# Eight sign levels instead of seven in the second quantiser, and the output copies moved from VectorE to ScalarE

## The reference, cut to what matters

```python
def _act_quant(x):
    scale = QB / jnp.maximum(jnp.max(jnp.abs(x), axis=-1, keepdims=True), EPS)   # QB = 127
    q = jnp.clip(jnp.round(x * scale), -QB - 1, QB) / scale
def _weight_quant(w):
    scale = 1.0 / jnp.maximum(jnp.mean(jnp.abs(w)), EPS)
    q = jnp.clip(jnp.round(w * scale), -1.0, 1.0) / scale
h = x * rsqrt(mean(x * x) + EPS) * w_norm
value, gate = split(_act_quant(h) @ _weight_quant(w_gv))     # hidden 8192 each
u = value * silu(gate)
out = _act_quant(u) @ _weight_quant(w_out)                   # 8192 -> 2048
x = layernorm(x + (x + out))                                 # w_norm is ones
```

## Time and profile before

| what | us |
|---|---|
| median of two runs | 7970.94 (7932.42 and 8009.45) |
| the profiled execution, its own time | 7965.22 |
| its span on the slowest core (core 6) | 7963.7 |
| spans of the other cores | 7869.0 to 7954.0 |
| VectorE busy / ScalarE busy / TensorE busy | 4085.7 / 3093.0 / 3355.5 |
| start of the last stage's first load of `ub2` | 5035.63 |

### The profile page before, as it was taken

The page is one execution under the profiler, slowest core; times in us unless marked ns, Lnnn a source line. Parts: engine busy times, 40 slices in busy tenths (PEclk is TensorE's granted clock), DMA queues, the critical chain, the costliest instruction groups (busy, mean ns, idle before and its releaser), DMA issues.

```text
span 7963.7 us, 48961 instructions; the slowest of 8 cores (7869.0 to 7963.7 us)
## 1 busy us (share of the span) xinstructions
PE 3355.5 (42%) x12882; PEld 1355.7 (17%) x13138; DVE 4085.7 (51%) x3369; ACT 3093.0 (39%) x3030; POOL 180.3 (2%) x343
## 2 busy tenths in 40 slices
PE   2100021120228888888889300000542715446186
PEld 0000000000014333333333100000210202112032
DVE  3600036658464444444444333677777676677612
ACT  2444421221323333333333455455554354354400
POOL 2000000000000000000000000000000000000000
PEclk7555555555569999999999655555765757667576
DMA  6776610010112222222222465112433415234232
GB/s 154 256 256 210 188 52 21 21 42 0 40 48 96 96 95 96 95 96 96 96 96 99 134 198 185 38 63 63 139 100 122 132 64 164 92 104 139 83 122 100
DMA packets 217460, 853.69 MB, mean 107 GB/s; under 512 B 34656, under 2 KB 34656, under 8 KB 159840
## 3 DMA queue, kind: packets, MB, share of 16 engines
q1 hardware_dynamic: 120240, 604.05, 22.7%
q10 hardware_dynamic: 64512, 167.80, 5.6%
q0 software_dynamic: 32432, 78.70, 4.1%
HBM read 694.24 MB, written 167.77 MB: 108 GB/s over the span
## 4 chain that ended last, share of the span: by engine, by line
DVE 45%; ACT 19%; DMA 17%; PE 8%; issue 6%; POOL 1%; ACTq 1%; DVEq 1%; SPq 0%; POOLq 0%
DVE zt L80 16%; DMA ub<-u_sp 5%; DMA wmean<-wgvt 5%; ACT wqt L80 4%; ACT wqs L80 4%; DMA wmean<-woutT 3%; PE pout L1323 3%; DVE res L80 3%; DVE paby L80 3%; ACT wabs L80 3%; DVE Mx L80 2%; DVE mq L80 2%; DVE o_ts L80 2%; DVE sg_t L80 2%; DVE gc_t L80 2%
## 5 line engine op out<-in xcount | busy, mean ns | idle before, releaser
L1323 PE MATMUL pout<-q_r,qo_r 128*128 128x512 bf16 x4012 | 1045.2, 428 | 1129.9 <-DMA qo_r<-qo_sp 598.5
L1017 PE MATMUL pvg<-q,qwv 128*128 128x512 bf16 x4014 | 1029.3, 412 | 378.4 <-DVE u_r L80 212.4
L80 DVE SCALAR_TENSOR_TENSOR zt<-mq,zt 128x1024 f32<-128x1024 f32 x768 | 941.2, 1225 | 138.6 <-DVE zt L80 136.8
L80 ACT ACTIVATE mq<-zt,pbh 128x1024 f32<-128x1024 f32 x768 | 881.9, 1148 | 197.2 <-DVE zt L80 194.8
L1022 PE MATMUL pvg<-q,qwg 128*128 128x512 bf16 x4014 | 928.9, 382 | 4.4
L1323 PEld LDWEIGHTS pout<-q_r,qo_r 128*128 128x128 bf16 x4096 | 437.6, 107 | 1741.5 <-issue 1635.3
L80 ACT ACT_TABLE_LOAD x77 | 98.8, 1283 | 1579.9 <-DVE q L80 404.3
L1017 PEld LDWEIGHTS pvg<-q,qwv 128*128 128x128 bf16 x4096 | 423.3, 104 | 954.4 <-issue 566.1
L80 ACT ACTIVATE wabs<-wmean 128x2048 f32<-128x2048 f32 (+1 forms) x256 | 379.6, 1483 | 473.3 <-DMA wmean<-wgvt 265.8
L1022 PEld LDWEIGHTS pvg<-q,qwg 128*128 128x128 bf16 x4096 | 402.8, 98 | 490.2 <-issue 29.5
L80 ACT ACTIVATE sg_t<-gc_t 128x512 f32<-128x512 f32 x256 | 161.2, 630 | 558.5 <-DVE gc_t L80 558.5
(11 more groups left out here) (146 smaller groups left out, 3889.6 us busy)
## 6 DMA issues: line engine op xcount, KB each, us to landing
wmean<-wgvt SPq DMA_DIRECT2D x128, 1024.0 KB, 6.0
wld<-wgvt SPq DMA_DIRECT2D x128, 1024.0 KB, 4.9
qo_r<-qo_sp SPq DMA_DIRECT2D x128, 1024.0 KB, 5.7
wmean<-woutT SPq DMA_DIRECT2D x128, 512.0 KB, 4.2
u_sp<-u_r ACTq DMA_DIRECT2D x64, 1024.0 KB, 4.4
wo_r<-woutT SPq DMA_DIRECT2D x128, 512.0 KB, 3.8
ub<-u_sp POOLq DMA_DIRECT2D x256, 256.0 KB, 5.3
qo_sp<-qo_t ACTq DMA_DIRECT2D x128, 256.0 KB, 2.9
```

The lines of the kernel that those rows point to most:

```text
L80: r = f(*a, **kw)
L1017: t.matmul(pvg[:, 2 * q * TS:(2 * q + 1) * TS], qwv[:, r * 2048 + k * 128:r * 2048 + (k + 1) * 128], q1[:, (ts * DC + k) * TS:(ts * DC + k ...
L1323: last = t.matmul(pout[:, d * TS:(d + 1) * TS], qo_r[:, base + d * 128:base + (d + 1) * 128], rhs, start=(j == 0), stop=(j == HC - 1))
```

## The change

Three edits, all in the last stage.

1. The level with weight 0.5 is done like the other seven: `HYB_S` gets an eighth weight, the loops run to 8, and VectorE's `tensor_scalar` (`is_ge`) and `tensor_tensor` (subtract) of each lane go. The bias of the copy to `q2c` changes from -1.0 to -0.5.
2. The eight copies `o_ts <- pout` of the first half are ScalarE's: the callback is called in ScalarE's program of the quantiser ahead of pair 8, and TensorE waits for ScalarE's semaphore.
3. The eight copies of the second half, in the epilogue, are ScalarE's as well; VectorE waits for them.

```diff
-    HYB_S = [-64.0, -32.0, -16.0, -8.0, -4.0, -2.0, -1.0]
+    HYB_S = [-64.0, -32.0, -16.0, -8.0, -4.0, -2.0, -1.0, -0.5]
...
             for p in range(NP):
-                if mid_cb is not None and p == NP // 2:
-                    mid_cb(v)
                 for lane in range(2):
...
-                for k in range(7):
+                for k in range(8):
                     for lane in range(2):
                         c0, c1 = lane * 2 * TS, (lane + 1) * 2 * TS
-                        v.wait_ge(sA.h, ab + 16 * p + 2 * k + lane + 1)
+                        v.wait_ge(sA.h, ab + 18 * p + soff(p) + 2 * k + lane + 1)
...
-                    v.tensor_scalar(out=mq2[:, c0:c1], in0=zt2[:, c0:c1],
-                                    scalar1=-0.5, scalar2=1.0,
-                                    op0=ALU.is_ge, op1=ALU.mult)
-                    v.tensor_tensor(out=zt2[:, c0:c1], in0=zt2[:, c0:c1],
-                                    in1=mq2[:, c0:c1], op=ALU.subtract)
...
         @SCA
         def _(sc, ts=ts, vb=vb, ab=ab):
             for p in range(NP):
-                vo = voff(p)
-                for k in range(7):
+                if mid_cb is not None and p == NP // 2:
+                    mid_cb(sc)
+                for k in range(8):
...
-                                  in_=mq2[:, c0:c1], func=AF.Copy, bias=-1.0)
+                                  in_=mq2[:, c0:c1], func=AF.Copy, bias=-0.5)
...
                 if dg == 1:
-                    t.wait_ge(sV.h, dg1_gate)
+                    t.wait_ge(sA.h, dg1_gate)
...
-        def cb(v):
-            v.wait_ge(sMM.h, f2_m0 + HC)
+        def cb(sc):
+            sc.wait_ge(sMM.h, f2_m0 + HC)
             if ts > 0:
-                v.wait_ge(sOut.h, 16 * DC * ts)
+                sc.wait_ge(sOut.h, 16 * DC * ts)
             for d in range(8):
-                v.tensor_copy(out=o_ts[:, d * TS:(d + 1) * TS],
-                              in_=pout[:, d * TS:(d + 1) * TS])
+                sc.copy(out=o_ts[:, d * TS:(d + 1) * TS],
+                        in_=pout[:, d * TS:(d + 1) * TS])
...
-        @VEC
-        def _(v, ts=ts, f2_m0=f2_m0):
-            v.wait_ge(sMM.h, f2_m0 + 2 * HC)
+        @SCA
+        def _(sc, ts=ts, f2_m0=f2_m0):
+            sc.wait_ge(sMM.h, f2_m0 + 2 * HC)
             for d in range(8):
-                v.tensor_copy(out=o_ts[:, (8 + d) * TS:(9 + d) * TS],
-                              in_=pout[:, d * TS:(d + 1) * TS])
-        tok_ev2 = sV.n
+                sc.copy(out=o_ts[:, (8 + d) * TS:(9 + d) * TS],
+                        in_=pout[:, d * TS:(d + 1) * TS])
+        tok_ev2 = sA.n
```

More of the change, by code:

```diff
@@ L1177, in emit_q2_slice, with soff @@
         vb, ab = sV.n, sA.n
-        def voff(p):
+        def soff(p):
             return 8 if (mid_cb is not None and p >= NP // 2) else 0
@@ L1182, in emit_q2_slice @@
             pp, lane = divmod(u, 2)
-            vfin[(ts, u)] = vb + 22 * pp + voff(pp) + 21 + lane
+            vfin[(ts, u)] = vb + 20 * pp + 19 + lane
         sl = slice(ts * TS, (ts + 1) * TS)
@@ L1228, in _ @@
                     c0, c1 = lane * 2 * TS, (lane + 1) * 2 * TS
-                    v.tensor_scalar(out=mq2[:, c0:c1], in0=zt2[:, c0:c1],
-                                    scalar1=-0.5, scalar2=1.0,
-                                    op0=ALU.is_ge, op1=ALU.mult)
-                    v.tensor_tensor(out=zt2[:, c0:c1], in0=zt2[:, c0:c1],
-                                    in1=mq2[:, c0:c1], op=ALU.subtract)
-                for lane in range(2):
-                    c0, c1 = lane * 2 * TS, (lane + 1) * 2 * TS
                     v.scalar_tensor_tensor(
@@ L1238, in _ @@
                         in1=ub2[:, c0:c1], op0=ALU.mult, op1=ALU.add)
-        assert sV.n == vb + 22 * NP + (8 if mid_cb is not None else 0)
+        assert sV.n == vb + 20 * NP
         @SCA
@@ L1243, in _ @@
             for p in range(NP):
-                vo = voff(p)
-                for k in range(7):
+                if mid_cb is not None and p == NP // 2:
+                    mid_cb(sc)
+                for k in range(8):
                     for lane in range(2):
                         c0, c1 = lane * 2 * TS, (lane + 1) * 2 * TS
-                        sc.wait_ge(sV.h, vb + 22 * p + vo
+                        sc.wait_ge(sV.h, vb + 20 * p
                                    + (1 + lane if k == 0 else 2 * k + 1 + lane))
@@ L1265, in _ @@
                         in_=q2c[:, lane * 1024:(lane + 1) * 1024]))
-        assert sA.n == ab + 16 * NP
+        assert sA.n == ab + 18 * NP + (8 if mid_cb is not None else 0)
     prev_next_ok = None
@@ L1374, in _ @@
             def _(g):
-                g.wait_ge(sV.h, _ev)
+                g.wait_ge(sA.h, _ev)
                 sLG.inc(g.dma_start(out=draw, in_=o_ts[:]), 16)
@@ L1380, in _ @@
         def _(v, tok_ev2=tok_ev2, tok_lb=tok_lb, c2sl=c2sl, ts=ts):
-            v.wait_ge(sV.h, tok_ev2)
+            v.wait_ge(sA.h, tok_ev2)
             v.wait_ge(sLb.h, tok_lb)
@@ L1486, in build_program @@
     for ts in range(NTS):
-        dg1_gate = sV.n + (22 * NP // 2 + 8 if ts + 1 < NTS else 8)
+        dg1_gate = sA.n + (18 * (NP // 2) + 8 if ts + 1 < NTS else 8)
         f2_m0 = emit_f2_loads_mms(ts, dg1_gate)
@@ L1491, in build_program, with _ @@
         else:
-            @VEC
-            def _(v, ts=ts, f2_m0=f2_m0, cb=mk_evdg0(ts, f2_m0)):
-                cb(v)
+            @SCA
+            def _(sc, ts=ts, f2_m0=f2_m0, cb=mk_evdg0(ts, f2_m0)):
+                cb(sc)
         emit_f2_epilogue(ts, f2_m0)
```

## The result

The changed kernel takes 7834.22 us, median of 11 runs (7810.64 to 7885.10), against 7914.71 us for the kernel before, median of 10 (7902.97 to 8009.45), two of which are the two shown ahead of the prediction. The ratio is 0.9891, with a 95% interval from 0.9854 to 0.9928. The forecast ratio was 7881 / 7965.2 = 0.9894. The forecast time, 7881, is 47 us too high, and its range (7838 to 7932) misses the measured median by 4 us.

A forecast was written before the change was run, and what follows sets the result against it. The prediction took a serial loop of VectorE's levels and a load per pair as the bound. Its terms, -93.4 + 0 + 8.0 + 1.5 = -83.9 us, took 7965.2 to 7881 us, range 7838 to 7932.

The forecast's parts named there:

- What bounds the kernel: Slice quantiser: a serial loop of VectorE's levels, then a load, over 64 pairs; idle time at the load 419.6 us.
- Part 1: Eighth sign level in the quantiser: 1.46 us saved a pair, 93.4 us over 64 pairs.
- Part 2: Copies moved to ScalarE in the middle of three slices: 0 us, bounds -0.4 and +2.4 for each.
- Part 3: Epilogue copies on ScalarE: 2.7 us later three times, +8.0; in the last product and last epilogue +0.75 each, +1.5.
- The sum: Whole kernel: -93.4 + 0 + 8.0 + 1.5 = -83.9 us.
- The level: Whole kernel: the profiled execution's 7965.22 us taken as the base from which the gain was subtracted, giving 7881.
- B: ScalarE's new duties cost more: table loads around the middles and a smaller eighth-level gain, 7898 us; chance 0.07.
- C: Bare last product: TensorE's clock stays lower after the longer pause, 82 us per half, 8045 us with both; chance 0.02.
- A: Quantiser loop: `ub` loads slowed by packed weight traffic; each landing 1.46 us later would give 7975 us; chance 0.06.
- One of my signs of being wrong: Last product: the prediction is wrong if its second half is not near 136 us.

The follow-up runs named there:

- both later groups: Two later sets of runs, each on one chip beside the unchanged kernel before, whose median was 7942.05 us (19 runs) and 7943.44 us (7 runs).

## Why the prediction was right and where it was wrong

**What bounds the kernel: right.** A serial loop of VectorE's levels and one load. Two buffers took the load out of it and 344 us with it.

**Part 1, -1.46 us a pair: right.** The two operations of the eighth level stand 1.40 apart as forecast, and `ACT mq` releases 3.1 us in 896 operations. That ScalarE's work costs nothing was a claim on 0.25 us of room; without the `Sign` a pair is 0.14 shorter, the hand-over alone.

**Part 2, the middles at 0: right.** 0.5 us won at slice 1's, no table load. The 0.2 I had worked out was too small because I took 0.72 us a copy from an early row; it is 0.66.

**Part 3, +2.7 per epilogue and +0.75 twice: right in kind, too large.** Measured +2.1 and +0.3, again from 5.30 us instead of 5.8 for eight copies. The five added loads are there, each with 1.28 us ahead of its copies. The Trainium skill ("ScalarE: Activation LUTs", "What ACT_TABLE_LOAD costs") adds a drain of about 1380 ns to the load for every switch of set. No such time shows in these rows: a copy begins 1.29 us after its load does, and in the epilogue the load begins 0.49 us after the end of `q2c`.

**The sum, -83.9 us: right, as far as it can be told.** The two comparisons of the changed kernel give 80.5 and 104.5 us less than the kernel before, ratios of 0.9891 and 0.9874; -83.9 of 7965 is 0.9895 and lies in both intervals. With the terms as the rows measured them (+2.1 three times, +0.3 twice, and three times the -0.5 that was read at slice 1's middle) the sum would have been -88.

**The level: wrong.** The step that failed is in the sum and the range: "The profiled execution took 7965.22 ... I say 7881", and then the range centred there, as the two runs "lie 39 us to either side of their median, and I have no reason for less around mine". The level was 50.5 us above the 7914.71 which ten runs of the kernel before gave, and the gain I took off was 3.4 us larger than the one measured there; the two leave the 47 us of error. The stated bounds are not what that working gives either: 39 us to either side of 7881 and of B's 7898 would be 7842 and 7937. What the level held was a stage at a reduced pace on two cores, and there was reason to see it in the views I had, the spans and mean granted clocks of the cores of that execution:

```profile
core 0: 7905.6 us, clock 0.693
...
core 4: 7896.7 us, clock 0.671
core 5: 7916.0 us, clock 0.671
core 6: 7963.7 us, clock 0.678
core 7: 7954.0 us, clock 0.679
```

Cores 6 and 7 stand 38 us and more above the other six. The mean clock does not tell them apart from cores 4 and 5; the row of the last product does, with 0.81. I read that row as the kernel's pace, mostly at the 2.4 GHz level with a start at 1.2, and built rival C on a further fall. It was a reduced pace already: core 6 stays at 0.81 in the stretch from 7800 to 7840 us, 151 matmuls in 40 us where core 4 does 187 at 1.00 from 7720 to 7760, and on the other six cores T was some 50 us shorter. Of those six the slowest is core 5, and 7916.0 + 1.5 - 83.9 = 7833.6 would have been the forecast, beside 7834.22 measured. That it meets it within a us is luck: the undisturbed profile taken later would have given 7929.3 - 83.9 = 7845.4 by the same rule, and in both later groups the median of the kernel before was 28 us above its first one. That part of the level I can't explain.

**The rivals.** A (the load takes it back): no. On the mean of the cores the wait is 416.4 and 426.9 us in the two profiles of before, 414.5 with the eighth level alone, and 428.6 and 438.8 in the two of the full change, where the loads of the middles are no longer behind VectorE's copies. B: no; there is no load in the middles, and the pace is 1.40. C: the pause grew to 6.98 us and the half after it ran at 0.99; refuted as an effect of this change, but what it fears, a lower granted clock in the bare last product, is what cost the profiled execution 50 us. One of my signs of being wrong came out by this: the second half of the last product was not near 136 us, but 109. The sign was wrong, since 136 was never the pace of the other six cores.

## What to carry to other kernels

When a prediction adds a difference to a measured level, look at the level core by core first: if one or two cores of the slowest execution stand apart in one stage, take the difference from the trace and the level from the cores that agree. An operation given to an engine that waits for its partner in every round cost the hand-over and no more here, where its 1.15 us plus hand-over fitted into a round of 1.40. And price a repeated wait from the row that groups all of them, not from the one seam that was opened: here 5.8 us against 4.8.

## What the runs showed of the hardware that I had not expected

In the last product, with all cores in the same dense matmuls, two cores of a die can be granted 0.81 of full speed while the other two of the same die are at 1.00. It was cores 6 and 7 in the profile of before and in the one with the epilogue's copies back, and cores 4 and 5 without the eighth `Sign` (0.83 on core 4, 308 matmuls in 80 us against 373 on core 6) and with two buffers (151 matmuls in 40 us on core 4 against 187 on core 6, 7280 to 7320 us). With the level alone it was cores 6 and 7 for the end of the product only (T 416 and 422). It costs 40 to 50 us of some 250 where it lasts. In the other profiles all eight cores ran that product at 0.91 to 1.00 in stretches of 40 us that hold no start or end of a half. The Trainium skill, "TensorE: Matmul & The Clock Gate", section "Seeing it yourself", describes a current limit that takes the whole die to 13/16 of the clock under dense matmuls. The value of 0.81 agrees. That it takes the whole die does not: here it took two cores of four.

The same lower clock costs nothing where the product is not what ends last. In F1, from 3000 to 3250 us of the profile of before, cores 4 and 5 are at 0.81 and do 954 matmuls; cores 0 and 1 are at 0.95 and 0.92 and do 935 and 949. So the mean clock of a core says little about its time; the stage in which it fell does.
